# One audio tower on one core: the order of the embedding, of the split of x and of the score maxima

## The reference

```
h  = layernorm(patches(x) @ W.T + b) * gamma + beta          # 124 tokens of 256 values per batch
xn = layernorm(h)
q, k, v = xn @ Wq.T + bq, xn @ Wk.T + bk, xn @ Wv.T + bv
h  = h + softmax(q @ k.T / scale) @ v
xn = layernorm(h)
rh = relu(xn @ router_w1 + router_b1)
p  = softmax(rh @ router_w2 + router_b2)                     # 6 experts
top_w, top_i = top_k(p, 2);  gates = softmax(top_w)
h  = h + sum over the two chosen experts of gate * expert(xn)   # relu(xn W1+b1), relu(. W2+b2), . W3+b3
```

## Time and profile before

| what | value |
|---|---|
| median of 3 runs | 1306.05 us (1305.42 to 1306.99) |
| the profiled execution | 1304.3 us, of which the span from first to last instruction is 1302.5 us |
| mean granted clock of TensorE | 0.981 of full speed |
| busy shares of the span | TensorE 94%, VectorE 81%, GpSimd 71%, ScalarE 64% |
| h (L1091) starts of rounds 5 to 16 | 113.85 to 324.22 us, 11 rounds, 19.12 us each |

### The profile page before, as it was taken

The page is one execution under the profiler, slowest core; times in us unless marked ns, Lnnn a source line. Parts: engine busy times, 40 slices in busy tenths (PEclk is TensorE's granted clock), DMA queues, the critical chain, the costliest instruction groups (busy, mean ns, idle before and its releaser), DMA issues.

```text
span 1302.5 us, 28239 instructions
## 1 busy us (share of the span) xinstructions
PE 1226.8 (94%) x7888; PEld 1076.0 (83%) x7888; DVE 1059.6 (81%) x3593; ACT 837.1 (64%) x1838; POOL 926.7 (71%) x740
## 2 busy tenths in 40 slices
PE   3899999999999989999879999999999999999994
PEld 3788888888888878888668898888888888888893
DVE  4689889989999989989688787878787877777783
ACT  1577667667667757756656666666767676666662
POOL 2127787788788777788878678677676767776776
PEclk8899999999999999999999999999999999999997
DMA  2234555544444434456568989776696787687755
GB/s 78 85 121 115 137 148 153 140 110 124 118 114 116 120 106 113 111 142 185 141 164 207 261 200 215 140 128 112 125 228 114 124 186 160 111 176 166 132 56 60
DMA packets 137192, 180.45 MB, mean 139 GB/s; under 512 B 38344, under 2 KB 103500, under 8 KB 137036
## 3 DMA queue, kind: packets, MB, share of 16 engines
q0 software_dynamic: 75456, 69.19, 32.7%
q1 hardware_dynamic: 60316, 108.67, 27.2%
q10 hardware_dynamic: 1264, 0.79, 0.2%
HBM read 159.01 MB, written 101.49 MB: 200 GB/s over the span
## 4 chain that ended last, share of the span: by engine, by line
PE 48%; DVE 1%; POOL 1%; ACT 1%; issue 1%; POOLq 0%; DMA 0%; DVEq 0%; ACTq 0%
PE bank L758 28%; PE bank L785 15%; PE bank L747 4%; POOL out L552 1%; PE bank L566 0%; PE bank L696 0%; ACT rec L869 0%; DVE h L1144 0%; PE bank L710 0%; DVE x_lo L1301 0%; DVE stats L1003 0%; POOLq L90 0%; DMA out<-yo,tail 0%; DVE h L1091 0%; ACT xn2T L885 0%
## 5 line engine op out<-in xcount | busy, mean ns | idle before, releaser
L552 POOL DMA_INDIRECT out<-yo,tail x268 | 434.5, 1621 | 168.1 <-issue 135.2
L503 POOL DMA_INDIRECT expert_rows<-rec,row_i x256 | 350.1, 1368 | 72.7 <-issue 65.5
L954 ACT ACTIVATE h2v<-bank,small 128x512 f32<-128x512 f32 x134 | 92.3, 690 | 206.9 <-PE bank L758 188.8
L785 PE MATMUL bank<-w_sb,h_hi 128*128 128x256 f32 x1072 | 208.7, 288 | 2.0 <-issue 2.0
L758 PE MATMUL bank<-x_hi,w_sb 128*128 128x512 f32 x536 | 177.6, 392 | 4.4 <-DVE x_lo L1301 4.4
L758 PE MATMUL bank<-h_hi,w_sb 128*128 128x512 f32 x536 | 177.1, 391 | 1.8 <-issue 1.8
L785 PEld LDWEIGHTS bank<-w_sb,h_hi 128*128 128x128 f32 x1072 | 171.3, 191 | 2.4 <-issue 2.4
L785 PE MATMUL bank<-w_sb,h_lo 128*128 128x256 f32 x536 | 151.4, 283 | 0.0
L918 ACT ACTIVATE xn<-h,nmr,rstd 124x256 f32<-124x256 f32 x128 | 66.4, 590 | 124.4 <-DVE nmr L1136 120.5
L758 PEld LDWEIGHTS bank<-x_hi,w_sb 128*128 128x128 f32 x536 | 101.3, 189 | 26.0 <-issue 4.8
L495 POOL TENSOR_TENSOR rstd<-vareps,neghalf 124x4 f32<-124x4 f32 x96 | 115.0, 1198 | 8.0
(11 more groups left out here) (190 smaller groups left out, 3141.0 us busy)
## 6 DMA issues: line engine op xcount, KB each, us to landing
w_sb<-split_weights SPq DMA_DIRECT2D x189, 512.0 KB
xg<-expert_rows SPq DMA_DIRECT2D x67, 530.0 KB
out<-h SPq DMA_DIRECT2D x32, 496.0 KB
split_weights<-half_w SPq DMA_DIRECT2D x36, 256.0 KB
small<-in_esmall SPq DMA_DIRECT2D x67, 134.0 KB
x_in<-in_x SPq DMA_DIRECT2D x32, 250.0 KB
expert_rows<-pad_rows SPq DMA_DIRECT2D x9, 530.0 KB
raw_w<-in_eweights SPq DMA_DIRECT2D x36, 128.0 KB
```

What stands on the lines that cost most here:

```text
L503: pool.indirect_dma_start(rows_dram, bass.IndirectOffsetOnAxis(ap=row_i[0:TOK, slot, j, k:k + 1], axis=0), rec[0:TOK, slot, j, :], None).t ...
L552: pool.indirect_dma_start(out, bass.IndirectOffsetOnAxis(ap=tail[:, t % TAILS, j, E8:].bitcast(I32), axis=0), yo[:, t % YO, j, :], None, c ...
L785: mm = pe.matmul(banks[6 + b][:, (j % 2) * D:(j % 2 + 1) * D], act[:, c, j * P:(j + 1) * P], w[:, 2, c, wh, :], start=(c == 0 and p == 0), ...
L954: act.activation(h2v[:, m, :], banks[4 + m][:], ACT.Relu, bias=small[:, t % SLOTS, DC + m:DC + m + 1]).then_inc(S["h2_v"], 1)
```

## The change

Three things move, and nothing is added or left out.

1. TensorE does the embedding of `x0` directly behind the transposes, and the scores of `x2` behind the embedding.
2. ScalarE's `xT_hi` and VectorE's `xT_lo` for a group are made one round earlier, in the stage `xs` (group `it + 1`). ScalarE makes it behind `gexp` and in front of `qT`; VectorE behind `rinv` and in front of `half_w`. The pipeline gets a round -1, in which only the first group's split is made, and SyncE loads `x` two groups ahead.
3. VectorE's `xn1T_lo` stands in front of `negmax`, which waits for the scores.

```
-            for it in range(G + DEPTH - 1):
+            for it in range(-1, G + DEPTH - 1):
                 straight(it)
...
-                if it + 1 < G:
-                    load_x(it + 1, (slot_it + 1) % RING)
+                if it + 2 < G:
+                    load_x(it + 2, (it + 2) % RING)
...
         @block.tensor
-                if x2:
-                    g, slot, rnd = x2
-                    pe.wait_ge(S["q_sb"], g * 2 + 2)
-                    bank_read(pe, (S["rh_sb"], it - 4, it - 3), (S["probs_ready"], it - 3, (it - 3) * GB + GB))
-                    ... the scores
-                if it == DRAIN:
-                    pe.wait_ge(S["v_ready"], G * 2)
-                    turn(0, 6)
                 if x0:
                     ... the embedding
                 if it == 0:
                     fold()
+                if x2:
+                    ... the scores, as above
+                if it == DRAIN:
+                    pe.wait_ge(S["v_ready"], G * 2)
+                    turn(0, 6)
...
         @block.scalar
-                x0, x1, x2, x3, x4 = (group_of(s) for s in range(DEPTH))
-                if x0:
-                    g, slot, rnd = x0
-                    act.wait_ge(x_loaded[slot], rnd * 16 + 16)
-                    wait(act, S["tok_ps"], g * 2)
-                    wait(act, S["xT_low"], g)
-                    act.activation(xT_hi[:], x_in[:, slot, :], ACT.Identity).then_inc(S["xT_high"], 1)
+                xs, x0, x1, x2, x3, x4 = (group_of(s) for s in range(-1, DEPTH))
...
                     act.activation(gexp[0:TOK, :], gap[0:TOK, :], ACT.Exp).then_inc(S["gate_exp"], 1)
+                if xs:
+                    ... the same four lines, for xs
...
         @block.vector
-                if x0:
-                    g, slot, rnd = x0
-                    v.wait_ge(S["xT_high"], g + 1)
-                    v.tensor_tensor(xT_lo[:], x_in[:, slot, :], xT_hi[:].bitcast(F32), ALU.subtract
-                                    ).then_inc(S["xT_low"], 1)
                 if x4:
                     probabilities(*x4)
...
-                if x2:
-                    g, slot, rnd = x2
-                    v.wait_ge(S["scores_ps"], g + 1)
-                    v.tensor_reduce(negmax[R, :], ...
                 if x1:
                     ... xn1T_lo
+                if x2:
+                    ... negmax, as above
...
                     v.reciprocal(rinv[R, :], probs[R, :, TOK]).then_inc(S["av"], 1)
 
+                if xs:
+                    g, slot, rnd = xs
+                    v.wait_ge(S["xT_high"], g + 1)
+                    v.tensor_tensor(xT_lo[:], x_in[:, slot, :], xT_hi[:].bitcast(F32), ALU.subtract
+                                    ).then_inc(S["xT_low"], 1)
                 for n in chunks_of(it):
```

More of the change, by code:

```diff
@@ L225, in chunks_of @@
         def chunks_of(it):
+            if it < 0:
+                return ()
             if it < FIRST_CHUNKS:
@@ L639, in step @@
                     fold()
+                if x2:
+                    g, slot, rnd = x2
+                    pe.wait_ge(S["q_sb"], g * 2 + 2)
+                    bank_read(pe, (S["rh_sb"], it - 4, it - 3), (S["probs_ready"], it - 3, (it - 3) * GB + GB))
+                    for j in range(GB):
+                        for c in range(DC):
+                            mm = pe.matmul(banks[5][0:TOK, j * TOK:(j + 1) * TOK], qT[:, c, j * TOK:(j + 1) * TOK],
+                                           xn1T[:, g % 2, c, j * TOK:(j + 1) * TOK], start=(c == 0), stop=(c == DC - 1))
+                    mm.then_inc(S["scores_ps"], 1)
+                if it == DRAIN:
+                    pe.wait_ge(S["v_ready"], G * 2)
+                    turn(0, 6)
                 if it == DRAIN + 1:
@@ L889, in step @@
                     act.activation(gexp[0:TOK, :], gap[0:TOK, :], ACT.Exp).then_inc(S["gate_exp"], 1)
+                if xs:
+                    g, slot, rnd = xs
+                    act.wait_ge(x_loaded[slot], rnd * 16 + 16)
+                    wait(act, S["tok_ps"], g * 2)
+                    wait(act, S["xT_low"], g)
+                    act.activation(xT_hi[:], x_in[:, slot, :], ACT.Identity).then_inc(S["xT_high"], 1)
                 if x1:
@@ L1052, in step @@
                                            op0=ALU.mult, op1=ALU.mult).then_inc(S["av"], 1)
-                if x2:
-                    g, slot, rnd = x2
-                    v.wait_ge(S["scores_ps"], g + 1)
-                    v.tensor_reduce(negmax[R, :], banks[5][R, 0:GT].rearrange("p (b k) -> p b k", b=GB), AX_X, ALU.max,
-                                    negate=True).then_inc(S["score_max"], 1)
                 if x1:
@@ L1063, in step @@
                                         ).then_inc(S["xn1T_low"], 1)
+                if x2:
+                    g, slot, rnd = x2
+                    v.wait_ge(S["scores_ps"], g + 1)
+                    v.tensor_reduce(negmax[R, :], banks[5][R, 0:GT].rearrange("p (b k) -> p b k", b=GB), AX_X, ALU.max,
+                                    negate=True).then_inc(S["score_max"], 1)
                 if x4:
```

## The result

The changed kernel takes 1346.91 us, the median of four runs (1346.36 to 1347.92), against 1305.74 us for the kernel before on the same chip (1304.41 to 1306.99). The ratio is 1.0318, with a 95% interval of 1.0304 to 1.0332: 41 us slower. The forecast was 1333 us with a range of 1322 to 1346, so the direction was right, 14 us of the loss were not in the forecast, and the time lies just outside the range. The profiled execution took 1347.92 us.

The account below looks back on a forecast made before the run. GpSimd's and VectorE's legs were taken to bound the 19.10 us round, then a loop through the scores at 19.94; the rounds' terms sum to +27 us on 1304.3, 1331, plus 1.75 for the median: 1333 us, range 1322 to 1346.

Parts of the forecast that it names:

- What bounds before: First part, 32 rounds: GpSimd's 10.18 us up to `h` plus VectorE's 8.92 us back make the 19.10 us round.
- GpSimd's leg: From VectorE's last statistics, through GpSimd's third `rstd`, four scatters and next first `rstd`, to `h`: 10.18 us.
- xT_lo at +0.59: VectorE's `xT_lo` moves into the stretch from `h` to the last statistics and adds 0.59 us a round there.
- Third rstd at -0.46: GpSimd's third `rstd`, no longer beside `xT_lo`, takes 1.05 us instead of 1.51.
- The scores' loop: A loop from `nmr` through embedding, scores, `negmax` and `h` decides: 19.94 us a round, +0.84; chance 0.66.
- up to 2.1: VectorE's new wait for the scores in front of `negmax`, in us, unless ScalarE's `xn1T_hi` hold up `xn1T_lo`.
- Rounds 0 to 4: Pipeline filling: rounds 0 and 1 cost 0, rounds 2 to 4 cost 1.25 us each, 3.8 in all.
- Round 23 and 24, and the second part: A slow clock behind 2.96 us idle costs round 23 +1.3 us; the second part keeps its length.
- The clock: TensorE's idle time before the transposes grows from 0.30 to about 1.15 us; granted clock stays, except around round 23.
- the rival: The clock falls in every round: +1.5 us or more on 23 rounds beyond the forecast, 1370 us; chance 0.05.
- The sum: All terms over the first part's rounds give +27 us; profiled execution 1331 us, predicted median 1333 us.

Follow-up runs that it names:

- e1_fill: The changed kernel with the v projection of the fourth batch computed twice, six matmul instructions more a round: 1337.08 us, ratio 1.0234.
- e6_rstd_twice: The kernel before, with GpSimd's third `rstd` computed twice and nothing moved: 1335.27 us, ratio 1.0231.
- e4_split_hidden: The kernel before with the early split of `x`, `xT_lo` between the embedding's statistics and `y`, `xT_hi` behind `probs`: 1298.9 us, ratio 0.9952.
- e5_split_in_wait: The changed kernel with `xT_lo` between `xn1T_lo` and `negmax` (except round 0) and `xT_hi` in front of `rec`: 1319.92 us, ratio 1.012.
- e2_split_only: The kernel before with the early split of `x` alone, TensorE's order and the place of `negmax` as before: 1311.5 us, ratio 1.0041.
- e10_hidden_again: e4_split_hidden measured once more, unchanged, beside e9_three_behind: 1298.3 us, ratio 0.9959 against the kernel before.
- e7_max_front: The changed kernel with the swap undone, `negmax` in front of `xn1T_lo` again: 1369.28 us, ratio 1.049.
- e9_three_behind: e4_split_hidden with GpSimd's eight scatters split 2, 3, 3 instead of 2, 2, 4 among its three norms: 1297.14 us, ratio 0.9939.

## Why the prediction had the loop right and the clock wrong

The distance from `nmr` to `nmr`, summed over stretches, in us. "Filled" is e1_fill, which is the changed kernel with its clock held:

```
rounds      before    forecast   after     filled
1 to 4       67.70     +3.75     +6.07     +4.90
5 to 22     344.59    +15.1     +24.64    +15.95
23, 24       41.22     +3.0      +2.87     +2.81
25 to 27     57.29     +2.5      +3.94     +2.98
28 to 30     56.36     +2.3      +5.74     +2.65
31           18.83     +0.2      +0.25     +0.25
sum         585.99    +26.9     +43.5     +29.5
```

- **What bounds before.** Right. e6_rstd_twice lengthens GpSimd's leg and all rounds follow; e4_split_hidden shortens it and they follow.
- **xT_lo at +0.59.** Right: 0.58 in e5_split_in_wait.
- **Third rstd at -0.46.** Right: 1.05 us. Missed beside it: a scatter that is 0.13 us longer, seen in e2_split_only, where GpSimd bounds.
- **The scores' loop.** Right: 8.18 for 8.19, `negmax` at 8.22, the cast 0.38 for 0.35, the round 20.00 for 19.94. The 0.06 make 1.4 us over 23 rounds. The wait in front of `negmax` is 1.15 us and not "up to 2.1", since ScalarE's `xn1T_hi` do hold `xn1T_lo` up, by 0.43; that changes nothing in the sum.
- **Rounds 0 to 4.** With the clock held, rounds 2 to 4 are 3.75 us longer, which is the forecast to the digit, but by luck: they gave 0.47, 1.52 and 1.76 us where 1.25 each was put. Round 1 was put at 0 and is 1.15 us longer. That is no more than one trace differs from another there: e4_split_hidden and e10_hidden_again are the same kernel, with 17.04 and 15.69 us in round 1.
- **Round 23 and 24, and the second part.** Right: 2.87 for 3.0, and 0.3 for 0.
- **The clock.** This is the step that failed. "TensorE's idle time in front of the transposes from 0.30 to about 1.15 us a round" was right (1.2 in most). What was drawn from it, "its clock stays", was not: the sum has the clock at nothing but for round 23. It rested on one idle time of 1.05 us, in round 30, which the prediction calls 29. That was a single case, in front of another instruction, in a kernel whose other idle times were short. And the rival was cut as all or nothing: every round or none. The trace shows nine of the steady rounds and round 3, 43.5 - 29.5 = 14.0 us. I gave it 0.05 at 1370 us and nothing in between.
- **The sum.** Between the two traces the rounds grow by 43.5 us where 26.9 were forecast: 14.0 of the 16.6 missing are the clock, 1.1 round 1, and the rest mostly the 0.06 a round. That the medians also miss by 14 is partly luck: the profiled execution of the changed kernel was the slowest of its four, by 1.0 us over the median, and the forecast had 1.75 added for the kernel before.

The Trainium skill, TensorE: Matmul & The Clock Gate, section "HAM oscillation — how this bites in real kernels", tells of a clock that cools at each wait between bursts; the waits of its example are of 3 to 5 us. Of long waits these traces agree: in each of the twelve the clock fell in round 24, behind 2.4 to 3.7 us. What they add is that waits of 0.9 to 1.5 us, once in each round, brought it down in nine of the steady rounds and left it in the others.

Still open: why round 15 fell and round 16, with a longer idle time in front, did not. With less of this idle time fewer rounds fell, down to none; no run tells which ones, nor what else than its length counts.

## What to carry to other kernels

Where a change makes TensorE wait about a microsecond in each turn of a loop, price its clock in between "never" and "always", and ask first whether TensorE's work lies on that loop: if not, the fallen clock can be free, as in e6_rstd_twice, and if so it costs in each fallen round what the slowed work loses, here 1.1 to 1.6 us. Before giving an instruction a new place, look where its engine already waits: the same `xT_lo` cost 0.58 us a round behind `rinv`, and gave a kernel 0.4 to 0.5% faster than the one before when it lay in the wait for `rstd`, with TensorE's old order.

## What the runs showed of the hardware

- **More work, less time.** Six useless matmul instructions a round made the kernel 9.8 us faster: they filled 0.7 us of TensorE's idle time, and the granted clock stayed at 1.00 in the nine rounds.
- **The cast is held by a scatter only if it starts late in it.** At 0.51 us into the scatter it took 0.17 us (e7_max_front), at 0.57 into it it took 0.71 (337.71 against 337.14) and 0.73 (e9_three_behind, 336.69 against 336.12), at 0.92 into it 0.38, and each held one ended with the scatter (341.99 + 0.38 = 342.37 beside 341.07 + 1.32 = 342.39). In all twelve traces, a cast that started up to 0.55 us into a scatter took 0.17 us, and one that started 0.56 to 0.96 us into it was held to its end. So a phase shift of a few hundredths of a microsecond changes it by 0.5 us.
- **A scatter that starts while xn1T_lo runs is longer.** In e2_split_only `xn1T_lo` ends at 340.08 + 1.25 = 341.33, 0.24 us behind the start of the second scatter, which takes 1.44 us; in the changed kernel it ends 0.18 us behind it (338.31 + 1.26 against 339.39), and the scatter takes 1.37; before, it ended just in front of it (335.87 + 1.25 against 337.14), and the scatter took 1.31. Single rounds with 0.40 and 0.56 us gave 1.60 and 1.75 (scatters at 546.20 in the changed kernel and at 625.39 in the kernel before). The first scatter of e2_split_only, in which `xn1T_lo` only begins, has the 1.43 us that the first one has everywhere. The Trainium skill, SBUF — State Buffer, section "Who interferes with whom", infers that a `tensor_tensor` with two SBUF inputs takes only the read side of the shared ports, and that descriptor generation needs the write side, so that the two don't disturb each other; these rows speak against that for a scatter that starts second.
